# Conditioned attention on one core: two more warm-up products, v products ahead of the first row maxima, and the low parts of the third group set apart

## The reference

```
Q = x @ Wq.T + bq ; K = x @ Wk.T + bk ; V = x @ Wv.T + bv        # 16 heads of 32
tQ = cond @ Wq.T + bq ; tK = cond @ Wk.T + bk
scores = (Q + tQ) @ (K + tK).T / sqrt(32)
out = x + softmax(scores) @ V
```

## Time and profile before

| | |
|---|---|
| median of three runs | 671.43 us (671.38 to 673.34) |
| profiled execution | 671.83 us, of which span of the profile 670.0 us |
| TensorE busy | 661.4 us, 99% of the span |
| VectorE, GpSimd, ScalarE busy | 538.9, 486.2 and 373.4 us |
| chain that ended last | 95% TensorE, 2% VectorE, 1% DMA, 1% ScalarE |

### The profile page before, as it was taken

The page is one execution under the profiler, slowest core; times in us unless marked ns, Lnnn a source line. Parts: engine busy times, 40 slices in busy tenths (PEclk is TensorE's granted clock), DMA queues, the critical chain, the costliest instruction groups (busy, mean ns, idle before and its releaser), DMA issues.

```text
span 670.0 us, 10084 instructions
## 1 busy us (share of the span) xinstructions
PE 661.4 (99%) x3550; PEld 447.7 (67%) x3550; DVE 538.9 (80%) x819; ACT 373.4 (56%) x659; POOL 486.2 (73%) x202
## 2 busy tenths in 40 slices
PE   8999999999999999999999999999999999999997
PEld 6776776666776666776666676666677666675442
DVE  4676888878888878888888888887988887887886
ACT  6435565556565555565555655555555555555572
POOL 5518777788777789777779777779777778766890
PEclk9999999999999999999999999999999999999999
DMA  7943334553434554434554334554334555235401
GB/s 234 254 105 90 92 94 129 143 143 97 116 96 121 143 142 115 106 99 111 142 143 123 101 101 107 141 144 126 97 111 95 142 127 123 79 94 136 128 33 48
DMA packets 48278, 79.87 MB, mean 119 GB/s; under 512 B 9826, under 2 KB 9826, under 8 KB 48226
## 3 DMA queue, kind: packets, MB, share of 16 engines
q1 hardware_dynamic: 47700, 79.21, 44.6%
q10 hardware_dynamic: 528, 0.02, 0.0%
HBM read 19.95 MB, written 8.39 MB: 42 GB/s over the span
## 4 chain that ended last, share of the span: by engine, by line
PE 95%; DVE 2%; DMA 1%; ACT 1%; SPq 0%; issue 0%; ACTq 0%
PE bank L273 26%; PE bank L373 19%; PE bank L352 18%; PE bank L393 17%; PE bank L329 13%; DVE mf L672 1%; PE bank L401 1%; DMA Ks<-lo 1%; PE bank L424 1%; DMA cT<-condT 1%; PE bank L302 0%; ACT Pt L583 0%; DVE lo L662 0%; ACT hi L561 0%; SPq L919 0%
## 5 line engine op out<-in xcount | busy, mean ns | idle before, releaser
L583 ACT ACTIVATE Pt<-bank 128x512 f32<-128x512 f32 x512 | 299.4, 601 | 228.9 <-PE bank L373 157.3
L672 DVE TENSOR_REDUCE mf<-bank 128x1 f32<-128x512 f32 x496 | 334.1, 686 | 103.2 <-PE bank L352 102.1
L859 POOL TENSOR_TENSOR A<-A,Pt 128x2048 f32<-128x2048 f32 x59 | 270.9, 4591 | 4.6
L373 PE MATMUL bank<-Qs,Ks 98*128 98x512 f32 x496 | 201.1, 407 | 0.9 <-ACT Pt L583 0.7
L352 PE MATMUL bank<-Ks,Qs 96*128 96x512 f32 x496 | 200.4, 404 | 1.5 <-DVE mf L672 0.7
L859 POOL TENSOR_TENSOR A<-Pt 128x2048 f32<-128x2048 f32 x30 | 138.4, 4612 | 3.1 <-DVE part_sums L697 2.0
L373 PEld LDWEIGHTS bank<-Qs,Ks 98*128 98x128 f32 x496 | 93.2, 188 | 59.9 <-ACT Pt L583 39.7
L833 POOL TENSOR_TENSOR Xl<-xr,Xh 128x512 fp32r<-128x512 f32 x28 | 36.1, 1291 | 119.1 <-ACT Xh L546 119.1
L393 PE MATMUL bank<-Pt,V 128*32 128x512 f32 x1024 | 116.9, 594 | 0.0
L352 PEld LDWEIGHTS bank<-Ks,Qs 96*128 96x128 f32 x496 | 93.7, 189 | 27.5 <-DVE mf L672 5.0
L273 PE MATMUL bank<-Xl,Wh 128*128 128x512 f32 x256 | 102.6, 401 | 0.0
(11 more groups left out here) (66 smaller groups left out, 376.1 us busy)
## 6 DMA issues: line engine op xcount, KB each, us to landing
Qs<-hi SPq DMA_DIRECT2D x62, 256.0 KB, 3.6
Ks<-hi SPq DMA_DIRECT2D x62, 256.0 KB, 3.6
Qs<-lo SPq DMA_DIRECT2D x31, 256.0 KB, 4.1
Ks<-lo SPq DMA_DIRECT2D x31, 256.0 KB, 4.0
xr<-xT SPq DMA_DIRECT2D x28, 256.0 KB, 2.7
res<-xT SPq DMA_DIRECT2D x28, 256.0 KB, 2.9
outT<-ot SPq DMA_DIRECT2D x28, 256.0 KB, 3.8
Qs<-mt SPq DMA_DIRECT2D x124, 4.0 KB
```

Source lines behind the costliest of these rows:

```text
L373: e.matmul(st_bank(u)[:, :], k[0:98, j, kc * P:(kc + 1) * P], q[0:98, j, :], start=True, stop=True).then_inc(t_st, 1)
L583: e.activation(exponentials(g)[:, kc, j, :], st_bank(u)[:, :], ACT.Exp, scale=SCALE).then_inc(a_e, 1)
L672: e.reduce_max(to[:, 4 * j + qc:4 * j + qc + 1], MXB[u % 2][:, :], AXX).then_inc(v_mx, 1)
L859: e.tensor_tensor(sums, ex[:, 0, :, :] if kc == 1 else sums, ex[:, kc, :, :], ALU.add).then_inc(p_a, 1)
```

## The change

`WARM` goes from 3 to 4: products of zeros (`res` by `res`, 256 columns) before the first real product. `warm_up_more` puts two more, of 64 columns, behind `condition(0, 0)`. `V_AHEAD` issues the first five products of `first` before the loop over u. On VectorE `qk_lo(0, 2)` moves into the loop behind `row_maxima(21)`, and `qk_lo(1, 2)` behind `row_maxima(25)`, the first of the loop over t; both stood between the two loops.

```
-WARM = 3
-K1_LO_AT = 2
+WARM, WARM_MORE, V_AHEAD = 4, 2, 5
+K1_LO_AT, Q2_LO_AT = 2, 21
...
+            def warm_up_more():
+                for i in range(WARM_MORE):
+                    e.matmul(MXB[0][:, 0:64], res[:, 0:P], res[:, 0:64], start=True, stop=True)
...
             warm_up()
             condition(0, 0)
+            warm_up_more()
...
-            done = 0
+            for k, g, n in first[:V_AHEAD]:
+                project(k, g, n)
+            done = V_AHEAD
...
+                if u == Q2_LO_AT:
+                    qk_lo(0, 2)
...
-            for qk in (0, 1):
-                qk_lo(qk, 2)
...
+                    if t == 0 and n == 0:
+                        qk_lo(1, 2)
```

## The result

The changed kernel is slower: 673.87 us median of 15 runs (672.72 to 677.2) against 671.55 us of 15 runs of the kernel before (670.56 to 673.34), a ratio of 1.0035 with a 95% interval of 1.0024 to 1.0046. The forecast was 670.9 us, the range ended at 671.9.

What follows compares the result with a forecast made beforehand. TensorE bounds the kernel, busy 99% of the span. Zeros 0, v products and low parts -1.8, 1.25 given back at the load: -0.55 from 671.83, so 671.3; median 0.4 lower: 670.9 us. Range 669.6 to 671.9.

Steps and rivals of the forecast that it cites:

- the path: Behind the load of `xr`, ScalarE's `x_hi(1,3)` starts at 51.6 instead of 52.18 us; TensorE is full from there.
- `maxima(27)` would come free: Near 45 us, `qk_lo(1,2)` no longer holds `maxima(27)`: about 44.5 instead of 46.23, where about 1.0 us were lost.
- the gain ahead of the load: V products and low parts bring `maxima(28)` 1.8 us earlier, 1.5 without the faster clock; ScalarE reaches `x_hi(1,3)` at about 50.0.
- the clock: In the opening, more zeros could end the 0.43 us pace before 9.6 us; q's projection would end about 0.7 us sooner.
- `Ks<-lo` still lands at 21.50: Group 0's last stack transfer keeps its landing, the DMA engines being saturated from 14.0 to 21.5 us; the zeros sum to 0.
- only the slack in it can go: In the chain to the load of `xr`, 43.4 to 52.1 us, only 0.55 us can be saved; 1.25 us are given back.
- Rival 3: Slower: a clock step after k's projection of group 0 makes `Ks<-lo` late; 673.4 us for a step at 13.3; 4%.
- rival 1: The clock doesn't rise earlier in the opening, so u = 19 and the load come later: -0.2 us, 671.2 us; 22%.
- Rival 2: The load of `xr` doesn't bind, so all 1.5 to 1.8 us stay: 669.6 to 669.9 us; 19%.
- rival 4: Nothing to see: `V_AHEAD` moves the wait by 0.3 us and the load gives all back: 671.4 us; 10%.
- The rule that the prediction weighed: TensorE's clock is held at half until activity releases it; by the page alone the opening would be 0.7 us shorter.
- The zeros' own sum: Before the condition's product, eight records at 0.43 us end at 4.78 us, 0.06 us after its 4.72 start.

Runs made afterwards that it cites:

- e1: The changed kernel run once more, nothing altered: 674.08 us against 672.42 us of the kernel before, ratio 1.003 (1.0015 to 1.0045).
- e2: The kernel before with only the five products of v issued ahead of the maxima: 674.22 us, ratio 1.0018 (1.0006 to 1.0029).
- e3: The kernel before with only the added zeros (4 and 2 small): 675.43 us, ratio 1.0036 (1.0024 to 1.0049), five runs.
- e4: The kernel before with only the two moved calls of `qk_lo`: 672.13 us, ratio 0.9994 (0.9983 to 1.0004).
- e5: The kernel before plus three products of zeros of 8 columns behind the three of 256: 674.14 us, ratio 1.0026 (1.0014 to 1.0038).
- e7: The changed kernel without its additional zeros: three products of 256 columns, none behind the condition; 672.6 us, ratio to the kernel before 1.001 (0.9997 to 1.0023).
- e9: The kernel before, unchanged, for a second profile: 672.25 us, ratio 0.9997 (0.9984 to 1.0009).
- e6: The changed kernel with its zeros as three products of 342 columns, none behind the condition: 672.55 us, ratio to the kernel before 1.0014 (0.9999 to 1.0029).
- e8: The changed kernel with the second sequence's fourth load issued ahead of the rows of maxima: 672.64 us, ratio to the kernel before 1.0009 (0.9997 to 1.0021).
- e10: The kernel before with only the second sequence's fourth load issued ahead of the rows of maxima: 671.09 us, ratio 0.9986 (0.9972 to 0.9999).
- e11: The kernel before with the low parts apart and the fourth load moved up: 671.13 us, ratio 0.9982 (0.9967 to 0.9996).
- e12: The changed kernel without its additional zeros and with the fourth load moved up: 671.77 us, ratio to the kernel before 0.999 (0.9977 to 1.0004).

## Why the prediction was wrong

**Right: the path.** The forecast said that the load of `xr` sets the result, since TensorE is full behind it. The start of `x_hi(1,3)` and that of the first `values` product, two stages on, in the profiles:

| kernel | `x_hi(1,3)` | `values` | difference |
|---|---|---|---|
| before | 52.18 | 62.56 | 10.38 |
| changed | 53.15 | 63.52 | 10.37 |
| changed again (e1) | 54.05 | 64.41 | 10.36 |
| v ahead alone (e2) | 52.62 | 63.00 | 10.38 |
| zeros alone (e3) | 54.00 | 64.37 | 10.37 |
| low parts alone (e4) | 52.15 | 62.54 | 10.39 |

Six profiles agree to 0.03 us, and so do those of e5, e7 and e9 (10.38, 10.39, 10.39); e6 is the exception, below. e8 and e10 to e12 show it from the other side: by the ratios, the one load moved is worth 0.8 to 1.4 us. That `maxima(27)` would come free was right too, though it came at 45.49, not 44.5, and so was the gain ahead of the load where nothing disturbed it: in e12 ScalarE comes to `x_hi(1,3)` at 49.99, where the forecast had 50.0. In the changed kernel it comes at 51.17 (53.15 - 1.98).

**Right, but not shown to be the zeros' doing: the clock.** The fast pace began at 6.3 us in both profiles of the changed kernel. It did so as early in profiles with the three old products of zeros, as here in e7:

```profile
5.14 0.73 PE L275 MATMUL bank<-Xh,Wh 128*128 128x512 f32 x1
5.71 0.40 PE L275 MATMUL bank<-Xl,Wh 128*128 128x512 f32 x1
5.95 0.39 PE L275 MATMUL bank<-Xh,Wl 128*128 128x512 f32 x1
```

e10, whose TensorE program is that of the kernel before, has it from 5.7 us too, and e3, with the added zeros, still has the slow pace at 10.42. The step moves from run to run by more than the zeros are shown to move it.

**Wrong: "`Ks<-lo` still lands at 21.50".** This was argued from saturated DMA engines, whose work the change leaves alone. It landed at 22.1, for the packet of instructions moved among its transfers. The landing also follows the first issue of the stack by 9.0 us, which the argument denied: the changed kernel issued it 0.74 us earlier (11.78 instead of 12.52) and by those 9.0 us would have had `Ks<-lo` at 20.8 without the packet. The kernel's own edits don't name that packet; twelve more records of TensorE were enough (10,096 instructions against 10,084). With it u = 19 and the rows of maxima came 0.6 us later, where I had 0, and `maxima(28)` came 0.7 us earlier (46.76 instead of 47.50), where I had 1.8; e12, without the packet, has 45.69.

**Wrong: "only the slack in it can go", -0.55 us.** The stack of q was issued at 42.82 instead of 42.19, 0.63 us later, and the load landed at 53.1 instead of 52.1, 1.0 us later, though issued at 47.37 instead of 47.72. The seven transfers fill the engines from 44 to 52 us, and most of that time move slower than before, where they had 260 to 287 GB/s between two slack stretches:

```profile
45.00:46.00 1.00, 1.00 (x5) 0.66 (x4) 1.00 (x2) 0.90 (x3) 0.00 (x0) 1.00 1.15 227
46.00:47.00 1.00, 1.00 (x5) 0.66 (x5) 1.00 (x3) 0.33 (x2) 0.00 (x0) 1.00 1.02 227
...
48.00:49.00 1.00, 1.00 (x6) 0.81 (x5) 0.55 (x1) 0.60 (x1) 0.00 (x0) 1.00 1.04 227
```

227 GB/s at a full share: filling the slack bought nothing, because the transfers together went slower. e4 says it without the late start: the stack of q issued at 41.70, 0.5 us earlier than before, the load landed at 52.1. Here the second profile of the kernel before (e9) has to be laid beside the first: it issued that stack at 41.81 and the load landed at 52.1 as well, 10.3 us later, where the first took 10.0. From that issue to the landing it took 10.3 in the changed kernel, 10.7 in e1 and 10.4 in e4; the forecast needed 9.4 (42.19 to 51.6). So the term was a gain of 0.55 us, measured it is 0.0 (e4), and with the late start a loss of 1.0 us. What slows the transfers is not settled. A second packet of instructions lies at 44.5 to 45.5 in all profiles, the kernel before's too, so it does not tell them apart.

**Missed: a second place.** `maxima(32)` needs the third group's stacks as well. Before, they landed at 51.5 and it was due at 52.23; now due at 51.5, it had to wait until 52.74. In the changed kernel the load hides this; in e8, where the load is out of the way, it is what remains (0.91 us lost, start to start). e12 has it too (0.73 us), e11 hardly (0.27 us). Whether this is why e12 is no better than e11 stays open: e12's profile reaches the first `values` product at 61.31 us, before e11's at 61.53. Another such wait comes with v ahead: TensorE then waits for `Qs<-mt` at the first scores (0.57 us lost in the changed kernel, 0.57 in e12), a wait that I did not list.

**Missed: a lower clock in some runs.** Of 27 runs of the changed kernel 5 list a mean granted clock of 0.994 or less, at 674.5 to 678.5 us; of 99 runs of the kernel before 2 list one below 0.996. A profile of e6 has 0.994 and shows where: TensorE loses 1.33 and 0.57 us between 51.0 and 54.2, and then works at half clock, the 1.2 GHz level, to 57.7 us (stretches, with the granted clock in the third column from the end):

```profile
50.00:52.60 2.60, 1.47 (x8) 0.85 (x6) 0.72 (x2) 0.90 (x2) 0.00 (x0) 1.00 0.64 136
...
54.00:55.00 1.00, 0.84 (x2) 0.73 (x3) 0.00 (x0) 0.71 (x3) 1.00 (x2) 0.65 0.00 0
55.00:56.00 1.00, 1.00 (x4) 0.75 (x3) 0.69 (x1) 0.48 (x1) 0.92 (x3) 0.50 0.00 0
56.00:57.00 1.00, 1.00 (x4) 0.81 (x3) 0.00 (x0) 0.00 (x0) 1.00 (x1) 0.50 0.00 0
...
650.00:655.00 5.00, 4.92 (x24) 2.16 (x27) 4.07 (x6) 4.46 (x9) 4.92 (x2) 0.66 0.14 52
```

From `x_hi(1,3)` to `values` it takes 11.90 us instead of 10.37. The page "TensorE: Matmul & The Clock Gate" of the Trainium skill, section "HAM oscillation — how this bites in real kernels", has the clock fall to half when waits leave the array idle. The rows of e6 agree, but e1 lost 1.50 and 0.68 us at the same two places, and e7 1.38 and 0.69, and both kept a granted clock of 1.00 from 54 to 58 us. So the waits alone don't decide it, and that they brought the lower clock to e6 is likely, not shown.

The other dip, 0.66 at 650 to 655 us among the last scores and values, is not of the change's making: runs with a mean clock of 0.997 are 47 of the 99 of the kernel before, at 672.9 to 673.2 on the average, against 671.5 to 672.0 for those at 0.999 or 1.0, some 1.3 us less. At equal clock the changed kernel stands 1.4 us above the kernel before in the set of e1 (673.39 against 671.97 at 0.999 and above, 674.59 against 673.24 at 0.997). The two profiles have `x_hi(1,3)` 0.97 and 1.87 us later than the first profile before. So of the 2.3 us about 1.4 are the late load; the rest is runs with a lower clock, of which some may lie behind the new waits. How much of that is chance of the runs stays open: of e2's 12 runs 10 stand at 0.997, of e12's with the same v products 4 of 12.

**The rivals.** Rival 3 had the place and the sign, a late `Ks<-lo`, but its cause, a late step of the clock, is absent from the changed kernel's two profiles (fast pace from 6.3 us in both), and so is that of rival 1; the one of e3 does have it, with the slow pace up to 10.8 us and a span of 673.6. Rival 2 fell with e4, where ScalarE waits for the load, and rival 4 with the result.

The rule that the prediction weighed, from the Trainium skill's page "TensorE: Matmul & The Clock Gate", section "What's actually happening", is not tested by these profiles, since the step came early and late under either warm-up; the earlier step gained nothing behind the wait for `Ks<-lo`. The zeros' own sum was 0.14 us short: the eight records end at 4.92 us (the last starts at 4.49), not at 4.78, and the condition's product starts at 5.05. It was of no account.

**What the zeros were for**, a longer warm-up, costs less with wider products than with one more (e6: 1.0014, 0.9999 to 1.0029), but is not worth having: e6 is no faster than the kernel before.

## What to carry to other kernels

Before an opening is filled with more work, ask which transfer ends the wait: here products were moved and added ahead of a DMA whose landing hung on the first issue of its row and on a packet of instructions, and what counted, 30 us later, was a load at the tail of a queue, to be had for one line in another place. Follow a saved microsecond to the next thing that is late and price that by its own landing, not by the slack before it. And where DMA engines are full, a few more instructions can have a cost beside their time: look for the instruction queue's packets when landings move for no reason, and try the same warm-up in wider products. Take more than one profile before you credit a change with something, like an early clock, that the old kernel may show as well.

## What was not expected of the hardware

- The profile lists packets of 16 KB on a queue of the kind "instruction", beside the data's. One packet keeps one DMA engine for 1.3 us (15.9% of 16 engines over 0.5 us). Amid the transfers of k it made `Ks<-lo` land some 1.2 us later (10.1 to 10.3 us after the stack's first issue instead of 8.9 to 9.1), in five profiles of five. With three products of 8 columns more it lay at 17.5 us, where the two profiles of the kernel before have it at 28.5 and 29.5. Whose instructions it holds the trace doesn't say: moving two calls on VectorE, and nothing on TensorE, went with a move to 25.0 (e4).
- If it falls a little later, it hits the next transfer: at 20.0 us in e6 and e7, `Ks<-lo` lands in time, and the weights behind it land 1.8 to 2.0 us after it (23.0 and 23.1 us) where the kernel before has 0.6; TensorE then loses 0.97 and 0.79 us ahead of `condition(0, 2)`. These are the profiles that took longer than the medians of their kernels, so a usual run of e6 or e7 may not have this wait.
- Seven 256 KB transfers ran at 253 GB/s from 43.4 to 50.6 us with gaps between the issues, and at about 229 GB/s from 44 to 52 us without.
